# The recurrence's loop on TensorE takes tiles 0 to 13, with an idle turn for the output of a tile that does not exist

## The chip, the cores and the metric

One program runs on one core of one Trainium2 chip. The metric is the device time of the program in microseconds, from start to end, as the median of several runs. TensorE does the matrix products, VectorE, ScalarE and GpSimd the element work, and SyncE (beside GpSimd and ScalarE) issues the transfers. The engines run programs of their own and meet at semaphores.

## The reference

A block of a metaformer: a normalisation over channels, chunked DeltaNet attention, a second normalisation, and a mixture of experts (8 experts, 2 for each token). The change touches the attention's recurrence alone. For each batch and head it is, over chunks of 16 tokens:

```python
def step(S, inp):
    qi, ki, vi, bi = inp
    kk = jnp.einsum('bhid,bhjd->bhij', ki, ki)
    T = eye + jnp.where(strict, bi[..., :, None] * kk, 0.0)
    rhs = bi[..., None] * (vi - jnp.einsum('bhcd,bhde->bhce', ki, S))
    U = jax.scipy.linalg.solve_triangular(T, rhs, lower=True)
    qk = jnp.einsum('bhid,bhjd->bhij', qi, ki)
    O = jnp.einsum('bhcd,bhde->bhce', qi, S) + jnp.einsum('bhij,bhje->bhie', jnp.where(incl, qk, 0.0), U)
    S_new = S + jnp.einsum('bhcd,bhce->bhde', ki, U)
    return (S_new, O)
```

followed by `y = o @ Wo`, and `t + y`. There are 8 batches, 12 heads of 16 channels, and 256 tokens, so 16 chunks.

## The kernel before, in words

The program has three stages. The first normalises, makes keys, values, queries and the triangular matrices, and inverts these. The second is the recurrence, from about 112 to 235 us in the profile below. The third routes the tokens and runs the experts, in 39 units of work of 128 rows.

The recurrence goes over NC = 16 tiles. A tile is one chunk of 16 tokens of all 8 batches, so 128 partitions, and the tiles depend on each other through the state. Each engine has its own loop over the tiles. All but TensorE's are written out by the program that builds the kernel, tile by tile; TensorE's is partly a loop on the engine.

One step of TensorE, `step(c, u, n)` (c the tile, u = c mod 2 the buffer, n = c div 2), does this in order:

- `w_state(c)` (line L1161) takes the state, turned by the triangular inverse, to PSUM bank 5. VectorE subtracts it and writes `uo` (L955).
- `w_and_u(c+1)` (L1131) is the next tile's product with the inverse.
- `turn_o(c-1)` (L1202), two transposes of the former tile's output `ow` into bank 7. ScalarE takes the high part of it as `oTh` (`o_high`, L1049), VectorE the rest as `oTl` (`o_low`, L935).
- `k_u(c)` (L1171) updates the state in banks 0 to 3, which VectorE masks into `s_sb` (L965).
- `output(c)` (L1179, L1185, L1192) makes the tile's output, which ScalarE takes out as `ow` (`o_in`, L1056).
- `turn_w(c+1)` (L1138, from `wx`), then `project(c-1)` (L1215), six products with the output weights `woh` and `wol`, added to the residual by VectorE (`y_in`, L941, and the statistics L944), then `turn_q(c+1)` (L1138, from `qx`).

Most of a step is small fp32 products: 12 in `w_state`, 48 in `w_and_u`, 12 in `k_u`, 12 and 48 in `output`. Each is two weight loads and two matmul instructions in the trace, so a step has 132 x 4 = 528 instructions for these, 30 for the turns, the zeroing product and the projection, and some waits.

Tiles 0 and 1 are written out ahead of the loop, since tile 0 has no former tile: `first(c)` leaves out its `turn_o` and `project`. The loop on the engine takes tiles 2 to 13, two a turn; tiles 14 and 15 are written out behind it. A wait in the loop compares a semaphore with a register that is worked out from the loop's counter.

Beside this, ScalarE and VectorE split the experts' weights into fp16 halves inside the tiles (`expert_high`, `expert_low`; two pieces of VectorE in tile 3, one in the later ones), and GpSimd inverts the second half of the triangular matrices. `wol` is made by GpSimd ahead of that (L861).

Of the kernel before, what the change touches and what calls it, by code (L numbers as in the profile page):

```python
# [22 lines left out]
NC = L // CH  # L23
# [27 lines left out]
WSCALE = 64.0  # L51
# [4 lines left out]
def program(nc, x, consts, wqkvb, wo, gate, wfc, bias, wproj, out):  # L56
# [4 lines left out]
    with ctx:  # L61
# [686 lines left out]
        with ExitStack() as scan:  # L748
# [38 lines left out]
            def o_bank(c):  # L787

                return 6 if isinstance(c, int) and c == NC - 1 else 7

            def rows_of(e):
# [12 lines left out]
            with nc.Block() as block:  # L804
# [88 lines left out]
                def _(dve):  # L893
# [37 lines left out]
                    def o_low(c):  # L931
                        dve.wait_ge(oh_done, c + 1)
                        if c >= 2:
                            dve.wait_ge(y_done, c - 1)
                        nc.vector.tensor_tensor(oTl[c % 2][:, :, :].rearrange("p a n -> p (a n)"), ps[0:HC, o_bank(c), 0:2 * TP],  # L935
                                                oTh[c % 2][:, :, :].rearrange("p a n -> p (a n)"), ALU.subtract)\
                            .then_inc(ol_done, 1)

                    def y_in(c):
                        dve.wait_ge(y_done, c + 1)  # L940
                        nc.vector.scalar_tensor_tensor(r_sb[:, c, :], ps[:, 7, 2 * TP:2 * TP + C], 1.0 / WSCALE, r_sb[:, c, :],  # L941
                                                       ALU.mult, ALU.add).then_inc(y_out, 1)
                        dve.wait_ge(y_out, c + 1)
                        nc.vector.bn_stats(st_sb[:, c, :], r_sb[:, c, :]).then_inc(bn_done, 1)  # L944

                    spread_m(0)
                    nc.vector.memset(s_sb[0][:, :, :, :], 0.0).then_inc(s_ready, 1)
                    spread_m(1)
                    for c in range(NC):
# [40 lines left out]
                def _(act):  # L990
# [54 lines left out]
                    def o_high(c):  # L1045
                        act.wait_ge(o_t, c + 1)
                        if c >= 2:
                            act.wait_ge(y_done, c - 1)
                        nc.scalar.activation(oTh[c % 2][:, :, :].rearrange("p a n -> p (a n)"), ps[0:HC, o_bank(c), 0:2 * TP],  # L1049
                                             ACT.Copy).then_inc(oh_done, 1)  # L1050

                    def o_in(c):
                        act.wait_ge(o_done, c + 1)
                        if c >= 2:
                            act.wait_ge(o_t, c - 1)
                        nc.scalar.activation(ow[c % 2][:, :], ps[:, 5, C:2 * C], ACT.Copy).then_inc(ow_done, 1)  # L1056
# [23 lines left out]

                    nc.scalar.activation(woh[:, :, :], wo_sb[:, :, :], ACT.Copy, scale=WSCALE)
                    nc.scalar.activation(wo_sb[:, :, :], wo_sb[:, :, :], ACT.Copy, scale=WSCALE).then_inc(wo_h, 1)
# [25 lines left out]
                def _(pe):  # L1108
                    def first(c):

                        return isinstance(c, int) and c == 0
# [41 lines left out]
                    def w_state(c, u, n):  # L1153
                        pe.wait_ge(s_ready, c + 1)
                        pe.wait_ge(w_out, c + 1)
                        if not first(c):
                            pe.wait_ge(ow_done, c)
                        for g in range(HG):
                            for bb in range(4):
                                rows = slice(32 * bb, 32 * bb + 32)  # L1160
                                last = nc.tensor.matmul(ps[rows, 5, g * GW:(g + 1) * GW], wT[u][:, g, rows],  # L1161
                                                        s_sb[u][:, bb, g, :], start=True, stop=True)
                        last.then_inc(ws_done, 1)
# [33 lines left out]
                    def turn_o(c, u, n):  # L1197
                        pe.wait_ge(ow_done, c + 1)
                        if not first(c) and o_bank(c) == 7:
                            pe.wait_ge(y_out, c)  # L1200
                        for hf in range(2):
# [4 lines left out]
                    def project(c, u, n):  # L1206
                        pe.wait_ge(ol_done, c + 1)
                        if first(c):
                            pe.wait_ge(wo_l, 1)
                        if o_bank(c) != 7:  # L1210
                            pe.wait_ge(y_out, c)
                        k = 0
# [11 lines left out]
                    def step(c, u, n, more=True):  # L1224
# [4 lines left out]
                        if more:  # L1229
                            w_and_u(*after)  # L1230
                        if not first(c):
                            turn_o(*former)
                        if more:
                            k_u(c, u, n)
                        output(c, u, n)
                        if more:
                            turn_w(*after)
                        if not first(c):
                            project(*former)
                        if more:  # L1240
# [11 lines left out]
                    turn_q(0, 0, 0)  # L1252
                    step(0, 0, 0)
                    step(1, 1, 0)
                    with pe.Fori(1, NC // 2 - 1) as r:
                        step(2 * r, 0, r)
                        step(2 * r + 1, 1, r)
# [566 lines left out]
```

## Time and profile before

| | us |
|---|---|
| median of 3 runs | 450.08 |
| lowest and highest | 446.82, 450.12 |
| the profiled execution | 451.87 |
| its span, first to last instruction | 450.1 |
| what lies around the span | 1.8 |

The profile is of one execution. Its mean granted TensorE clock is 0.860 of full speed. The engines' busy times in it are 373.6 us (83%) for TensorE, 283.4 us (63%) for VectorE, 190.0 us (42%) for ScalarE and 241.7 us (54%) for GpSimd. Times below are microseconds from the span's start. A row of a timeline gives the start, the length, the engine, the line and the operation with its tiles and count; in brackets stands how long the engine was idle ahead of it, and what ended that. "issue" is a wait for nothing that the profile shows.

### The profile page before, as it was taken

To read this page: it belongs to the slowest core of one execution; us is meant where nothing else is said; L and a number is where in the kernel's file an instruction comes from. 1 tells how busy PE (TensorE), PEld (TensorE's weight loads), DVE (VectorE), ACT (ScalarE), POOL (GpSimd) and SP (SyncE) were. 2 spreads that over 40 slices of the span, in tenths; PEclk is the share of its full clock that TensorE was granted. 3 is DMA by queue.
4 is the path that set the end of the run, shared out by engine and by line. 5 is a ranking of instruction groups with operands and counts; after the bars stand their busy time and mean duration, and the time that the engine had idled before them with its cause. 6 is when DMAs were issued, how large, how long until landed. Compare 5 with 4: busy or idle time off the path is not lost. (4 is left out here: it accounts for less than half of the span.)

```text
span 450.1 us, 20125 instructions
## 1 busy us (share of the span) xinstructions
PE 373.6 (83%) x8144; PEld 293.3 (65%) x8144; DVE 283.4 (63%) x627; ACT 190.0 (42%) x444; POOL 241.7 (54%) x285
## 2 busy tenths in 40 slices
PE   3989898873878999999945827899999999999970
PEld 1556666541756787777724513699899998987750
DVE  5696679874445657788655888265756757555440
ACT  4576777421446678777624510133133131321110
POOL 3432336993499615554505303447878778676221
PEclk9998999855865589999985558699999999999895
DMA  7934236493626327787302401214333343334110
GB/s 234 298 134 147 105 119 160 139 275 116 122 82 183 103 77 221 221 250 243 113 1 72 181 35 26 57 28 54 63 58 52 62 58 60 46 44 53 18 22 9
DMA packets 39313, 48.85 MB, mean 109 GB/s; under 512 B 12790, under 2 KB 34886, under 8 KB 39000
## 3 DMA queue, kind: packets, MB, share of 16 engines
q1 hardware_dynamic: 29370, 30.34, 22.2%
q0 software_dynamic: 9488, 16.52, 18.3%
q10 hardware_dynamic: 400, 1.23, 1.0%
q8 instruction: 38, 0.62, 0.6%
q14 instruction: 17, 0.14, 0.1%
HBM read 30.05 MB, written 16.45 MB: 103 GB/s over the span
## 5 line engine op out<-in xcount | busy, mean ns | idle before, releaser
L1750 POOL DMA_INDIRECT out<-yo,give x39 | 68.6, 1759 | 45.7 <-DVE yo L1722 32.6
L1604 PE MATMUL ps<-xs,w_up 128*128 128x256 f16 (+1 forms) x552 | 77.9, 260 | 3.8 <-ACT xb L1663 2.3
L1663 ACT ACTIVATE xb<-xs 64x256 f16<-64x256 f16 (+1 forms) x23 | 8.8, 384 | 127.4 <-DVE xs L1687 127.4
L1604 PEld LDWEIGHTS ps<-xs,w_up 128*128 x552 | 53.1, 98 | 13.7 <-issue 4.9
L1729 POOL DMA_INDIRECT row<-d_x,take x39 | 39.6, 1015 | 33.8 <-DVE take L1451 22.2
L1722 DVE TENSOR_SCALAR yo<-ps,slot_gate 128x192 f32<-128x192 f32 x39 | 14.8, 414 | 51.8 <-PE ps L1624 51.8
L1714 DVE TENSOR_TENSOR hl<-hw,hh 128x512 f16<-128x512 f32 (+1 forms) x69 | 42.3, 614 | 2.4
L1624 PE MATMUL ps<-pjh,hh 128*128 x234 | 42.7, 249 | 0.4 <-DVE hl L1714 0.4
L1624 PE MATMUL ps<-pjh,hl 128*128 x234 | 42.4, 248 | 0.0
L1624 PE MATMUL ps<-pjl,hh 128*128 x234 | 42.4, 248 | 0.0
L1604 PE MATMUL ps<-xb,w_up 66*128 66x256 f16 (+1 forms) x138 | 36.1, 262 | 0.0
L1674 ACT ACTIVATE hw<-ps 128x512 f32<-128x512 f32 (+1 forms) x69 | 31.3, 514 | 7.0 <-PE ps L1604 7.0
L1712 DVE CAST hh<-hw 128x512 f16<-128x512 f32 (+1 forms) x69 | 28.1, 407 | 2.8 <-ACT hw L1674 2.8
L399 POOL TENSOR_TENSOR sqw<-kvw 128x384 f32<-128x384 f32 x8 | 6.6, 828 | 36.2 <-ACT beta L474 29.7
L705 PE MATMUL ps<-kqT 16*32 16x64 f32 x1536 | 20.5, 237 | 4.4 <-issue 3.2
L705 PEld LDWEIGHTS ps<-kqT 16*32 16x32 f32 x1536 | 16.8, 107 | 11.1 <-issue 10.7
L663 PE MATMUL ps<-wqh,tTh 96*128 96x384 f16 (+1 forms) x64 | 21.0, 328 | 3.4 <-DVE tTl L555 1.9
L1624 PEld LDWEIGHTS ps<-pjh,hh 128*128 128x128 f16 x234 | 20.5, 99 | 4.6 <-issue 3.9
L639 PE MATMUL ps<-wqh 96*128 96x512 f16 x49 | 15.9, 458 | 7.3 <-ACT wqh L447 7.3
L935 DVE TENSOR_TENSOR oTl<-ps,oTh 96x256 f16<-96x256 f32 x16 | 6.7, 421 | 23.9 <-ACT oTh L1049 23.9
L1624 PEld LDWEIGHTS ps<-pjh,hl 128*128 128x128 f16 x234 | 21.7, 99 | 0.0
L1624 PEld LDWEIGHTS ps<-pjl,hh 128*128 128x128 f16 x234 | 21.6, 99 | 0.0
(252 smaller groups left out, 939.6 us busy)
## 6 DMA issues: line engine op xcount, KB each, us to landing
d_kv<-kvw SPq DMA_DIRECT2D x8, 384.0 KB, 2.5
d_pt<-w_up SPq DMA_DIRECT2D x16, 192.0 KB, 2.7
kvt<-d_kv SPq DMA_DIRECT2D x16, 192.0 KB, 4.0
pt<-d_pt SPq DMA_DIRECT2D x16, 192.0 KB, 3.6
pjs<-wproj POOLq DMA_DIRECT2D x5, 576.0 KB, 6.6
fcs<-wfc POOLq DMA_DIRECT2D x6, 384.0 KB, 4.9
w_up<-wfc SPq DMA_DIRECT2D x4, 384.0 KB, 5.4
d_q<-qw SPq DMA_DIRECT2D x8, 192.0 KB, 2.7
```

Of the source, the lines that this page charges most:

```text
L639: nc.tensor.matmul(ps[:, bank, :], wqh[:, 0, 0:TP], wqh[:, 0, 0:512], start=True, stop=True)
L663: last = nc.tensor.matmul(ps[:, bank, 0:width], ts[u][:, j, hf, :], ws[:, hf, first:first + width], start=(k == 0), stop=(k == 5))
L705: last = nc.tensor.matmul(ps[cols, 4 + q, 64 * a:64 * a + 64], kqT[j][rows, a, 0, cols], kqT[j][rows, a, :, cols], start=True, stop=True)
L1604: last = nc.tensor.matmul(ps[:, NP * u + m // 2, (m % 2) * n:(m % 2 + 1) * n], w[k][:, m * 128:(m + 1) * 128], x, start=(k == 0), stop=(k ...
L1624: last = nc.tensor.matmul(y[half], hs[u][:, m // 2, at:at + TP], ws[:, m * C:(m + 1) * C], start=False, stop=(m == HB - 1 and k == 2), ski ...
L1663: nc.scalar.activation(xb[s % 2][0:64, 0:width(s)], xs[s % 2][0:64, width(s):2 * width(s)], ACT.Copy).then_inc(xb_in, 1)
L1674: nc.scalar.activation(hw[u][:, i, 0:2 * width(s)], ps[:, NP * u + i, 0:2 * width(s)], ACT.Gelu_apprx_tanh, scale=1.0 / WSCALE).then_inc(h ...
L1712: nc.vector.tensor_copy(hh[u][:, i, 0:n], hw[u][:, i, 0:n]).then_inc(hh_done, 1)
L1714: nc.vector.tensor_tensor(hl[u][:, i, 0:n], hw[u][:, i, 0:n], hh[u][:, i, 0:n], ALU.subtract)\
L1722: nc.vector.tensor_scalar(yo[s % YB][:, half, :], ps[:, 6, half * C:(half + 1) * C], slot_gate[:, at:at + 1], None, ALU.mult).then_inc(yo_ ...
L1729: nc.gpsimd.indirect_dma_start(row[s % RB][:, half, :], None, d_x.rearrange("p t c -> (p t) c"), bass.IndirectOffsetOnAxis(ap=take[:, at:a ...
L1750: nc.gpsimd.indirect_dma_start(out, bass.IndirectOffsetOnAxis(ap=give[:, at:at + 1], axis=0), yo[s % YB][:, half, :], None, compute_op=ALU ...
```

## The change

TensorE's loop takes tiles 0 to 13 in seven turns in place of tiles 2 to 13 in six; nothing of the recurrence is written out ahead of it. So that tile 0 can run the same instructions as the others, it does `turn_o` and `project` for a tile "-1": two transposes of zeros and six products of zeros, whose result nobody reads. VectorE clears `ow[1]`, `oTl[1]` and `oTh[1]` for it ahead of tile 0. Four semaphores start two higher (TURN = 2), and the counts that others wait for on `o_t` and `y_done` are one higher. TensorE waits for the clearing and for `wol` once, ahead of the loop. The order of the work in a step, and all other engines' loops, stay.

```diff
+            oh_clear = of("oh_clear")
+            TURN = 2
...
                     def o_low(c):
                         dve.wait_ge(oh_done, c + 1)
-                        if c >= 2:
-                            dve.wait_ge(y_done, c - 1)
+                        if c >= 1:
+                            dve.wait_ge(y_done, c)
...
                     def y_in(c):
-                        dve.wait_ge(y_done, c + 1)
+                        dve.wait_ge(y_done, c + 2)
...
-                        dve.wait_ge(y_out, c + 1)
+                        dve.wait_ge(y_out, TURN + c + 1)
...
                     nc.vector.memset(s_sb[0][:, :, :, :], 0.0).then_inc(s_ready, 1)
+                    nc.vector.memset(ow[1][:, :], 0.0).then_inc(y_out, TURN)
+                    nc.vector.memset(oTl[1][:, :, :], 0.0).then_inc(ol_done, TURN)
+                    nc.vector.memset(oTh[1][:, :, :], 0.0).then_inc(oh_clear, 1)
                     spread_m(1)
...
                     def o_high(c):
-                        act.wait_ge(o_t, c + 1)
-                        if c >= 2:
-                            act.wait_ge(y_done, c - 1)
+                        act.wait_ge(o_t, c + 2)
+                        if c >= 1:
+                            act.wait_ge(y_done, c)
...
-                        if c >= 2:
-                            act.wait_ge(o_t, c - 1)
+                        if c >= 1:
+                            act.wait_ge(o_t, c)
...
-                    nc.scalar.activation(woh[:, :, :], wo_sb[:, :, :], ACT.Copy, scale=WSCALE)
+                    nc.scalar.activation(woh[:, :, :], wo_sb[:, :, :], ACT.Copy, scale=WSCALE).then_inc(ow_done, TURN)
...
                         pe.wait_ge(w_out, c + 1)
-                        if not first(c):
-                            pe.wait_ge(ow_done, c)
+                        pe.wait_ge(ow_done, TURN + c)
...
                     def turn_o(c, u, n):
-                        pe.wait_ge(ow_done, c + 1)
-                        if not first(c) and o_bank(c) == 7:
-                            pe.wait_ge(y_out, c)
+                        pe.wait_ge(ow_done, TURN + c + 1)
+                        if o_bank(c) == 7:
+                            pe.wait_ge(y_out, TURN + c)
...
                     def project(c, u, n):
-                        pe.wait_ge(ol_done, c + 1)
-                        if first(c):
-                            pe.wait_ge(wo_l, 1)
+                        pe.wait_ge(ol_done, TURN + c + 1)
...
-                        if not first(c):
-                            turn_o(*former)
+                        turn_o(*former)
...
-                        if not first(c):
-                            project(*former)
+                        project(*former)
...
-                    step(0, 0, 0)
-                    step(1, 1, 0)
-                    with pe.Fori(1, NC // 2 - 1) as r:
+                    pe.wait_ge(oh_clear, 1)
+                    pe.wait_ge(wo_l, 1)
+                    with pe.Fori(0, NC // 2 - 1) as r:
                         step(2 * r, 0, r)
                         step(2 * r + 1, 1, r)
```

## Rows read from the trace of the kernel before

**Rows 1.** The page's 40 slices: granted TensorE clock in tenths of full speed.
```profile
PEclk9998999855865589999985558699999999999895
```

**Rows 2.** Stretches cut at clock changes: us, busy (instructions) by engine, PEclk, DMA.
```profile
116.00:122.70 6.70, 5.30 (x221) 4.26 (x224) 2.42 (x4) 4.03 (x12) 2.98 (x5) 1.00 0.64 116
...
129.50:133.00 3.50, 2.65 (x128) 2.00 (x127) 2.26 (x3) 2.55 (x8) 3.34 (x3) 0.99 0.02 5
133.00:160.20 27.20, 24.75 (x715) 20.19 (x715) 16.44 (x25) 15.51 (x35) 20.36 (x22) 0.50 0.45 133
160.30:218.40 58.10, 54.84 (x2672) 44.99 (x2674) 43.53 (x81) 44.16 (x109) 30.12 (x48) 1.00 0.72 215
```

**Rows 3.** Timeline of TensorE in tiles 0 and 1; idle before, and its releaser, in brackets.
```profile
121.49 0.33 PE L1171 MATMUL ps<-uo,kx 32*128 32x64 f32 x3 [0.62 <-issue]
...
124.93 0.69 PE L1138 MATMUL ps<-cst,wx 128*128 128x128 f32 x2 [0.88 <-issue]
126.29 0.88 PE L1138 MATMUL ps<-cst,qx 128*128 128x128 f32 x3 [0.67 <-ACT wT L1035]
...
133.21 0.50 PE L1192 MATMUL ps<-uo,pt 32*32 32x16 f32 x19 [0.94 <-issue]
```

**Rows 4.** Timeline of TensorE in tiles 2 to 5: tile starts and idle places.
```profile
136.07 0.87 PE L1161 MATMUL ps<-s_sb,wT 128*32 128x64 f32 x24
...
139.10 0.64 PE L1131 MATMUL ps<-kvt,mb 32*32 32x32 f32 x28 [1.05 <-issue]
...
144.21 0.84 PE L1192 MATMUL ps<-uo,pt 32*32 32x16 f32 x48 [0.69 <-issue]
...
147.41 0.87 PE L1161 MATMUL ps<-s_sb,wT 128*32 128x64 f32 x24
...
149.49 0.97 PE L1131 MATMUL ps<-kvt,mb 32*32 32x32 f32 x55 [0.49 <-issue]
...
157.25 0.87 PE L1161 MATMUL ps<-s_sb,wT 128*32 128x64 f32 x24
...
164.10 0.54 PE L1161 MATMUL ps<-s_sb,wT 128*32 128x64 f32 x24
```

**Rows 5.** DMA queues carrying instructions: all of them in 136.1:157.25, then in 157.25:218.3.
```profile
q8 instruction: 5, 0.08, 1.6%
...
q14 instruction: 5, 0.04, 0.2%
```

**Rows 6.** Timeline of TensorE in tiles 5 to 7: tile ends and starts at full clock.
```profile
169.59 0.52 PE L1138 MATMUL ps<-cst,qx 128*128 128x128 f32 x3 [0.17 <-ACT wT L1035]
170.20 0.54 PE L1161 MATMUL ps<-s_sb,wT 128*32 128x64 f32 x24
...
175.85 0.52 PE L1138 MATMUL ps<-cst,qx 128*128 128x128 f32 x3 [0.17 <-ACT wT L1035]
176.30 0.54 PE L1161 MATMUL ps<-s_sb,wT 128*32 128x64 f32 x24
```

**Rows 7.** Timeline of TensorE in tile 1: turn and projection of tile 0, at half clock.
```profile
129.33 0.83 PE L1202 MATMUL ps<-cst,ow 128*96 128x128 f32 x2
...
134.34 0.37 PE L1215 MATMUL ps<-woh,oTh 96*128 96x192 f16 x1
...
135.30 0.85 PE L1138 MATMUL ps<-cst,qx 128*128 128x128 f32 x3
```

**Rows 8.** Timeline of VectorE and GpSimd ahead of tile 0.
```profile
112.41 0.70 DVE L947 MEMSET s_sb<- 128x768 f32 x1
...
113.36 1.15 DVE L904 TENSOR_TENSOR mb<-mtc,cst 128x384 f32<-128x384 f32 x1
...
112.35 1.74 POOL L861 TENSOR_TENSOR wol<-wo_sb,woh 96x384 f16<-96x384 f32 x1 [0.52 <-ACT wo_sb L1082]
```

**Rows 9.** Timeline of VectorE in tile 3: the piece that other odd tiles lack.
```profile
154.57 0.94 DVE L918 SCALAR_TENSOR_TENSOR w_up<-w_up 128x768 f16<-128x768 f32 x1
```

**Rows 10.** Timeline of TensorE in the last tile.
```profile
229.66 0.26 PE L1192 MATMUL ps<-uo,pt 32*32 32x16 f32 x9 [1.15 <-issue]
```

More of the change, by code:

```diff
@@ L1206, in project @@
                     def project(c, u, n):
-                        pe.wait_ge(ol_done, c + 1)
-                        if first(c):
-                            pe.wait_ge(wo_l, 1)
+                        pe.wait_ge(ol_done, TURN + c + 1)
                         if o_bank(c) != 7:
-                            pe.wait_ge(y_out, c)
+                            pe.wait_ge(y_out, TURN + c)
                         k = 0
```

## The prediction

> **What bounds the kernel now.** I read the page's clock line first, then stretches of the recurrence cut where the clock changes, then TensorE's timeline tile by tile, then the queues that carry instructions. In the 40 slices the clock shows fives inside the recurrence, in the slices from about 124 to 158 us [rows 1]. The cut stretches give it sharply: full speed from 116.0 to 122.7, full again from 129.5 to 133.0 (half between the two), then half for 27.2 us to 160.2, and full for the remaining 58 us [rows 2]. These are the two levels, 1.2 and 2.4 GHz. TensorE is busy 24.75 of the 27.2 us at half clock and 54.84 of the 58.1 at full, so it is the bound of the recurrence in both, and a tile costs what its instructions cost: 6.10 us at full clock (164.10 to 170.20 to 176.30) [rows 4, 6], but 11.34 for tile 2 and 9.84 for tile 3 [rows 4].
>
> Tiles 2 and 3 hold another thing: three places where TensorE stands still for 1.05, 0.69 and 0.49 us with "issue" as the reason, in the middle of a run of equal products [rows 4]. Tiles 0 and 1 have three such, of 0.62, 0.88 and 0.94 [rows 3]. From tile 4 to tile 13, in the same instructions, I find none. What changes at tile 4 is that the loop on the engine takes its second turn. And the queue named q8, which carries instructions, moves 5 packets during tiles 2 and 3 and none at all during tiles 4 to 13; the 5 packets of that later stretch are q14's, of another size [rows 5]. 0.08 MB in 5 packets is 16 KB each; and between two idle places, 139.10 and 144.21 [rows 4], the timeline has 28 + 2 + 24 + 1 + 24 + 48 = 127 matmuls with as many weight loads, 254 instructions and a few waits. So my reading: the first time TensorE runs through code, it must be brought in block by block, and it waits at the ends of blocks; in later turns the code is there. The change runs tiles 2 and 3 from code that tiles 0 and 1 brought in.
>
> **The change part by part.** I sum against the profiled execution (span 450.1, time 451.87) and carry the difference to the median, 1.79 lower.
>
> *The three waits of tiles 2 and 3 go:* 1.05 + 0.69 + 0.49 = 2.23 us [rows 4]. All of it is on the path, since TensorE runs back to back around them. The waits of tiles 0 and 1 stay, as the first turn now goes through the same number of instructions for the first time; their places move by a few instructions, and I take them at the same 2.44 us in all [rows 3].
>
> *The clock.* Without the waits tile 2 at half clock is 11.34 - 1.74 = 9.60 us, and tile 3 is 9.84 - 0.49 = 9.35; at full it is 6.10, so each tile is about 3.3 us dearer at half. In this trace the clock rose at 160.3, 10.8 us after the last of the idle places ended at 149.49, with TensorE busy without a break in between [rows 2, 4]. That is the one row that tells how soon it rises in this sort of work, and I take it: the last idle place of the first turn ends near 133.9 (133.21 and 0.7 for the idle turn below), so the clock rises near 144.7. Tile 2 starts at 136.07 + 0.7 = 136.8 and does 7.9 of its 9.60 us at half, the rest (18%) at full in 1.1, and ends at 145.8. Tile 3 runs at full: 6.1, and 0.9 because there VectorE becomes late: it has one more piece of expert weights (0.94 us) than in the other odd tiles, where it has no slack left [rows 9]. That ends at 152.8, and tile 4 at 158.9. Before, tile 5 began at 164.10 [rows 4]. That is 5.2 us earlier, with the 2.23 and the 0.7 in it. Bounds: clock at full from the start of tile 2 gives 136.8 + 6.1 + 7.0 + 6.1 = 156.0, so 8.1 earlier; clock rising at 160.3 as before gives 136.8 + 9.60 + 9.35 = 155.75, then 4.55 us at half (48% of a tile) and 3.15 at full, so 163.45 and 0.65 earlier.
>
> *The idle turn in tile 0.* Two transposes: 0.83 us at half clock in tile 1 [rows 7], and as they stand in tile 0 behind `w_and_u`, near 120 and thus at full clock [rows 2], half of it, 0.4. They delay `k_u` and all behind it. The six products take 135.30 - 134.34 = 0.96 us at half clock [rows 7]; in tile 0 they fall into the 0.67 us in which TensorE waits for ScalarE's `wT` [rows 3], so 0.3 is left. Together 0.7, between 0.4 (products hidden) and 1.8 (nothing hidden, all at half).
>
> *Three clearings on VectorE.* The one of `s_sb`, four times the size of `ow`, takes 0.70 us [rows 8]; so three at less than 0.25 each, 0.7 at most. They push `spread_m(1)`, which ends at 114.51 [rows 8] and is wanted by `w_and_u(1)` behind the 0.54 us of `w_state(0)` at about 118.7. Four us of slack hide them. If that cover were gone they would cost their 0.7. Nobody else is queued behind them before tile 0; SyncE's loads of the inverse for tile 3 wait for `mb_done` and are wanted two tiles later.
>
> *Waits ahead of the loop.* TensorE now waits for `wol` before tile 0, and all of the recurrence is queued behind that. `wol` is done at 112.35 + 1.74 = 114.09 [rows 8] and TensorE gets there at 118.2, so it costs nothing; it would from 4.1 us of lateness on. `ow_done`'s first count comes from ScalarE's very first operation. The waits of ScalarE and VectorE name one count more and start from one more: the same moments.
>
> *One more jump back.* From tile 5 to 6, with a jump between, 0.61 us pass between the start of the last turn and the next tile; from 6 to 7, without, 0.45 [rows 6]. So +0.16 for the seventh turn's jump; the set-up of the counter moves from ahead of tile 2 to ahead of tile 0 at no price.
>
> *Behind the recurrence.* TensorE's program is two tiles shorter, so all later block ends fall elsewhere. One wait of this kind, 1.15 us, lies in the last tile, where nothing covers it [rows 10]: it may vanish, or another come. I count 0, and 1.2 either way for the range. What follows (statistics, routing) waits for the last tile's residual, so the gain goes through to the end.
>
> The Trainium skill, Runtime: NRT & Kernel Launch, section Instruction fetch mechanics, gives TensorE 2048 instructions in blocks of 256, which agrees with the 16 KB packets and idle places here, but calls the crossing of a block "mostly hidden". By that rule the 2.23 us would be no waits for code and would not go, and the sum would be a small loss; the rows differ, with up to 1.05 us at a crossing. The same section warns that a taken branch whose target is outside a window of two blocks forces a new fetch. The trace disagrees: the loop spans more than four blocks, and its jumps bring no packet.
>
> Sum: -5.2 + 0.16 = -5.0 on the span. 451.87 - 5.0 - 1.79 = **445.1 us**.
>
> **The rivals.**
> *The clock rises early, or never falls.* For it: at 129.5 it rose while idle places of 0.88 and 0.67 lay only 3 to 5 us back [rows 2, 3]. Against: 27 us at half with small waits only. -8.1 + 0.16 = -7.9: 442.2.
> *The clock rises when it did before.* For it: tiles 3 and 4 kept TensorE busy for 10 us and it stayed at half. Only 0.65 - 0.16 = 0.5 is left: 449.6.
> *The waits are not of the code's first pass,* or come again in tiles 2 and 3. Then nothing goes and the idle turn and the jump stay: +0.9, 451.0. Against: the packets of q8 [rows 5].
> *The clock is lost in tiles 0 and 1 too.* This is the one on the slower side. Before, 4.5 us of tile 0 (118.2 to 122.7) and 3.5 of tile 1 ran at full [rows 2]; at half they cost 8.0 x 9.5 / 6.1 = 12.4, so 4.4 more. With a rise as late as after tile 4, tile 5 begins at 136.8 + 4.4 + 9.60 + 9.35 + 9.35 = 169.5, or 5.4 later: with the jump +5.6, 455.6. It decides once the half clock holds from tile 0 beyond the middle of tile 4; up to there the gain covers it. For it: the idle turn leaves the waits of the first tiles as they are. Against: it adds work where TensorE stood idle.
> *Every turn fetches its code again.* This is the skill's branch rule as a mechanism of this kernel: the loop's first block has been overwritten at the jump. Each of the six later turns would have the 2.23 us: 13.4 - 2.2 + 0.9 = +12, 462. Against: the five jumps of before, over the same body, moved nothing on q8 [rows 5]. Only the place of the block ends in the body differs.
>
> **How the numbers follow.** Forecast 0.45; early clock 0.20; clock as before 0.20; waits stay 0.05; clock lost 0.07; fetched again 0.03. The range of 441.5 to 450.8 takes in the first four with the tail's 1.2 at most of them, and leaves out the last two and some ends. A difference under 1%, 4.5 us, can hardly be told from none. The forecast itself is on the faster side of that in 0.6 of its cases: faster 0.27 + 0.20 = 0.47; slower 0.10; the rest, 0.43, within 1%.
>
> **What would show it.** Right: no "issue" over 0.2 us in tiles 2 to 13, q8 silent from the first jump on, the same two or three idle places in tiles 0 and 1, the clock at full some 11 us after the last of them, tile 5 near 159. In tile 0 two transposes and six products that cost under 1 us together. Wrong: idle places in tile 2, packets on q8 in later turns, or a clock that stays at half past 150. Then the sign may still be right but the size not. A clock that differs from run to run would make the one profile a poor guide to the median.

## The result, and the profile after

The changed kernel took 448.14 us in the median of 20 runs (445.03 to 451.34), the one before 450.33 in 20 runs of its own (446.82 to 453.75). The ratio is 0.9954, with an interval of 0.9932 to 0.9976: faster, by 1.9 us in the profiled executions (450.01 against 451.87) and by 2.2 in the medians. Forecast were 5.0. The sign was right, and the time lies inside the range; the size was not. At half a per cent the difference is also below the 1% that the prediction called hardly to be told from none; that it is real rests on the same sign in four pairs of kernels (below).

The timeline of TensorE in the changed kernel, tile starts (`w_state` is now at L1165) and idle places, answers to [rows 3, 4]:

```profile
117.66 0.87 PE L1165 MATMUL ps<-s_sb,wT 128*32 128x64 f32 x24
...
124.69 0.29 PE L1196 MATMUL ps<-uo,pt 32*32 32x16 f32 x4 [1.53 <-issue]
...
130.88 0.42 PE L1136 MATMUL ps<-kvt,mb 32*32 32x32 f32 x11 [1.35 <-issue]
...
138.08 0.87 PE L1165 MATMUL ps<-s_sb,wT 128*32 128x64 f32 x24
...
145.92 0.54 PE L1165 MATMUL ps<-s_sb,wT 128*32 128x64 f32 x24 [0.76 <-DVE s_sb L970]
...
148.35 0.63 PE L1206 MATMUL ps<-cst,ow 128*96 128x128 f32 x2 [0.92 <-DVE r_sb L943]
...
155.18 0.87 PE L1165 MATMUL ps<-s_sb,wT 128*32 128x64 f32 x24
...
162.16 0.54 PE L1165 MATMUL ps<-s_sb,wT 128*32 128x64 f32 x24
...
216.41 0.54 PE L1165 MATMUL ps<-s_sb,wT 128*32 128x64 f32 x24
```

And in the kernel before, the starts of tile 0 and tile 14:

```profile
118.23 0.54 PE L1161 MATMUL ps<-s_sb,wT 128*32 128x64 f32 x24
...
218.37 0.54 PE L1161 MATMUL ps<-s_sb,wT 128*32 128x64 f32 x24
```

From tile 2 to tile 13 no idle place with the reason "issue" is longer than 0.22 us: the 2.23 us are gone. In tile 3 TensorE now waits for VectorE instead, 0.76 us at its start for the masked state and 0.92 for the residual. The tile lengths are what is new: tiles 0 and 1 took 138.08 - 117.66 = 20.42 us, and before 136.07 - 118.23 = 17.84. Tiles 2 and 3 took 17.10 against 21.18 [rows 4]. From the start of tile 0 to that of tile 5 it is 44.50 us against 45.87, so 1.4 us of gain, where the forecast has 5.2.

The queues that carry instructions, in tiles 2 to 13 (answers to [rows 5]), have nothing of q8 left:

```profile
q14 instruction: 5, 0.04, 0.2%
```

The stretches of the changed kernel, cut at tile 2 and where the clock changes (stretch, its us, busy and count for TensorE, its loads, VectorE, ScalarE, GpSimd, then granted clock, DMA share and GB/s), answer to [rows 2]:

```profile
117.70:138.10 20.40, 17.51 (x562) 14.47 (x561) 7.56 (x12) 9.47 (x25) 18.08 (x19) 0.58 0.26 66
138.10:148.20 10.10, 8.39 (x400) 6.91 (x399) 6.66 (x9) 8.89 (x20) 9.78 (x10) 0.84 0.80 241
148.20:158.40 10.20, 10.05 (x289) 8.19 (x292) 7.86 (x13) 5.40 (x16) 7.85 (x8) 0.50 0.21 59
158.50:216.40 57.90, 54.84 (x2664) 45.05 (x2663) 43.37 (x81) 43.87 (x108) 30.57 (x48) 1.00 0.74 216
```

The granted clock was at 0.58 of full over tiles 0 and 1 (0.72 before), at full from 141.4 to 148.2 (0.84 over that row), at half again for ten us in which TensorE was busy 10.05 of 10.20 us, and then full to the end of tile 13. Before, the 27.2 us at half were one piece. So the clock did come up earlier, 10.5 us after the last idle place ended at 130.88, much as forecast. What the forecast did not have is that it fell again, beside the waits for VectorE. That these brought it down is argued from their place, not shown.

VectorE in tiles 2 to 4 of the changed kernel:

```profile
142.06 0.42 DVE L937 TENSOR_TENSOR oTl<-ps,oTh 96x256 f16<-96x256 f32 x1 [2.63 <-ACT oTh L1054]
142.40 1.27 DVE L900 TENSOR_TENSOR mtc<-mtc,beta 128x192 f32<-128x192 f32 x1
143.70 1.22 DVE L906 TENSOR_TENSOR mb<-mtc,cst 128x384 f32<-128x384 f32 x1
144.84 0.94 DVE L970 TENSOR_TENSOR s_sb<-ps,cst 128x768 f32<-128x768 f32 x1
145.71 0.96 DVE L924 SCALAR_TENSOR_TENSOR w_up<-w_up 64x768 f16<-64x768 f32 x1
146.59 1.34 DVE L926 SCALAR_TENSOR_TENSOR pjl<-pjl,pjh 128x1152 f16<-128x1152 f32 x1
147.86 0.34 DVE L943 SCALAR_TENSOR_TENSOR r_sb<-ps,r_sb 128x192 f32<-128x192 f32 x1
...
148.52 0.34 DVE L960 TENSOR_TENSOR uo<-ub,ps 128x192 f32<-128x192 f32 x1
...
151.91 1.34 DVE L920 SCALAR_TENSOR_TENSOR w_up<-w_up 128x768 f16<-128x768 f32 x1
...
156.41 0.34 DVE L960 TENSOR_TENSOR uo<-ub,ps 128x192 f32<-128x192 f32 x1
```

In tile 2 it stands idle for 2.63 us until `oTh` is there. Then it spreads the triangular matrices (`mtc` and `mb`, 1.27 and 1.22 us) before it comes to the state, which TensorE waits 0.76 us for. Behind that stands one expert piece of two parts (0.96 and 1.34 us), and only then the residual, which TensorE waits 0.92 us for. So `uo` of tile 3 comes at 148.5, 2.6 us after the tile's start; in the later tiles the same takes 0.7 to 1.7 (from 162.16 to 162.83 in tile 5). Both waits in tile 3 thus stand behind VectorE's work of tile 2, which itself began late because of `oTh`. The extra piece in tile 3 (1.34 us at 151.91), which the prediction had priced, held TensorE up by nothing that shows.

The last two tiles are the other place of the difference. From the start of tile 14 to the reciprocal behind the statistics pass 232.05 - 216.41 = 15.64 us, before 235.21 - 218.37 = 16.84. First the reciprocal of the changed kernel, then that of the kernel before:

```profile
232.05 0.25 DVE L991 RECIPROCAL rstd<-rstd 128x16 f32<-128x16 f32 x1 [0.37 <-ACT rstd L1110]
```

```profile
235.21 0.25 DVE L986 RECIPROCAL rstd<-rstd 128x16 f32<-128x16 f32 x1 [0.37 <-ACT rstd L1105]
```

The 1.15 us of [rows 10] are gone, and tile 14 is as long as it was (6.77 and 6.82). By the reciprocal the changed kernel is 3.16 us ahead, 0.57 of it from ahead of tile 0 and 2.6 from the recurrence; 1.26 us of it are lost again in the routing stage, ahead of the gate's scores, where the one long piece is a transfer: the chain that ended last holds it at `d_x`, 3.69 us in the changed kernel and 1.61 before, at the same spot. First the chain of the changed kernel (start, us, what):

```profile
246.28 3.69 DMA d_x<-x
```

The same chain of the kernel before:

```profile
250.53 1.61 DMA d_x<-x
```

I take that for chance of the one execution: from the reciprocal to the end of the span it is 215.9 us in this profile, 214.2 in the second profile of the same kernel, and 214.9 and 215.3 in the two of the kernel before. What is said below of sizes goes by medians.

### The profile page after: what moved, and what is told of

Same layout as the page of the kernel before. It is cut to its first block and busy times, and to the rows that moved or that the text cites. A ratio compares the mean times of both kernels' runs of the same rounds, so it can differ in the third digit from the quotient of the medians.

```text
span 448.0 us, 20168 instructions
## 1 busy us (share of the span) xinstructions
PE 372.3 (83%) x8152; PEld 292.9 (65%) x8152; DVE 285.3 (64%) x630; ACT 189.9 (42%) x444; POOL 244.0 (54%) x285
## 3 DMA queue, kind: packets, MB, share of 16 engines
q0 software_dynamic: 9488, 16.52, 18.6%
## 5 line engine op out<-in xcount | busy, mean ns | idle before, releaser
L639 PE MATMUL ps<-wqh 96*128 96x512 f16 x49 | 16.9, 481 | 7.2 <-ACT wqh L447 7.2
```

The lines of the kernel that those rows point to most:

```text
L639: nc.tensor.matmul(ps[:, bank, :], wqh[:, 0, 0:TP], wqh[:, 0, 0:512], start=True, stop=True)
```

## The experiments

All ratios are to the kernel before on the same chip. The table has the medians; the columns of tiles are us in the one profiled execution of each, from tile start to tile start, "tail" is from the start of tile 14 to the reciprocal behind the statistics, and "all" is from the start of tile 0 to that reciprocal (tiles 6 to 13, not shown, take 48.0 to 48.5 us in every kernel). In names, +64, +128 and +192 are instructions of padding, explained below. The profiled execution need not be a typical one: it was the fastest of its runs, 2 to 5 us under the median, in the second profile of before, "four tiles written out", +192, "+128, piece later" and "piece earlier".

| kernel | median | ratio (95%) | tiles 0, 1 | 2, 3 | 4, 5 | tail | all |
|---|---|---|---|---|---|---|---|
| before | 450.33 | | 17.84 | 21.18 | 12.95 | 16.84 | 116.98 |
| before, second profile | 451.07 | 1.0041 (1.0011 to 1.0071) | 18.90 | 18.98 | 12.25 | 17.37 | 115.65 |
| after | 448.14 | 0.9954 (0.9932 to 0.9976) | 20.42 | 17.10 | 13.16 | 15.64 | 114.39 |
| after, again | 446.89 | 0.9925 (0.9895 to 0.9955) | 20.28 | 17.09 | 12.49 | 16.25 | 114.18 |
| idle turn alone | 451.50 | 1.0036 (1.0007 to 1.0064) | 20.05 | 18.95 | 12.74 | 17.92 | 117.75 |
| four tiles written out | 456.87 | 1.0149 (1.0096 to 1.0202) | 18.68 | 19.04 | 19.51 | 16.52 | 122.22 |
| after, piece later | 446.26 | 0.9926 (0.9890 to 0.9961) | 20.70 | 15.21 | 12.39 | 16.13 | 112.50 |
| after, 12 products | 447.16 | 0.9957 (0.9923 to 0.9990) | 20.67 | 16.78 | 12.42 | 16.02 | 113.95 |
| before, 12 products | 450.03 | 1.0013 (0.9984 to 1.0042) | 20.49 | 18.78 | 12.88 | 17.38 | 117.68 |
| after, +64 instructions | 447.23 | 0.9934 (0.9905 to 0.9964) | 18.43 | 15.82 | 13.16 | 17.84 | 113.33 |
| after, +128 | 445.63 | 0.9915 (0.9888 to 0.9942) | 15.29 | 13.41 | 15.31 | 19.22 | 111.28 |
| after, +192 | 448.29 | 0.9974 (0.9940 to 1.0007) | 17.81 | 15.17 | 13.15 | 15.34 | 109.53 |
| before, +128 | 450.39 | 1.0025 (0.9989 to 1.0062) | 16.11 | 22.68 | 12.95 | 15.69 | 115.60 |
| after, +128, piece later | 444.21 | 0.9873 (0.9830 to 0.9917) | 14.75 | 15.51 | 12.75 | 17.06 | 108.16 |
| after, piece earlier | 445.22 | 0.9924 (0.9892 to 0.9955) | 20.38 | 14.91 | 12.58 | 15.31 | 111.36 |
| after, piece earlier, +128 | 444.29 | 0.9903 (0.9869 to 0.9937) | 14.73 | 14.52 | 12.57 | 18.66 | 108.64 |

The second profile of before is the very same program, and came out 0.4% off itself with an interval that leaves out 1. So I take differences of under about half a per cent between two of these kernels for undecided, whatever their intervals. The sign of the change does not hang on one such difference: after against before is worth 0.46%, 0.75%, 0.56% (both with 12 products) and 1.1% (both with +128), and "all" is 114.39 and 114.18 us against 116.98 and 115.65.

### The changed kernel again

> The changed kernel itself once more, beside the kernel before. Theory (waits for code removed, part of the gain spent again): ratio 0.995, between 0.992 and 0.998, no idle place with reason issue above 0.3 us in tiles 2 to 13. Rival (the difference of the two profiles is where the clock happened to change, nothing of the program): ratio 1.000.

0.9925. With the first measurement the change is worth 0.5 to 0.75%, 2 to 3.4 us. In tiles 2 to 13 no idle place with the reason "issue" is over 0.2 us, and TensorE waits 1.49 us for VectorE's state at the start of tile 3. The rival (ratio 1.000) is out.

### The idle turn alone

```diff
-                    with pe.Fori(0, NC // 2 - 1) as r:
+                    step(0, 0, 0)
+                    step(1, 1, 0)
+                    with pe.Fori(1, NC // 2 - 1) as r:
```

> The changed kernel with tiles 0 and 1 written out again ahead of the loop, so that only the idle turn and the shifted counts are left of the change. Theory: the waits of tiles 2 and 3 are back (3 places, 2 to 2.5 us in all, 5 packets on q8 in tiles 2 and 3), and the idle turn costs 0.4 to 1 us: ratio 1.001 to 1.003. Rival (the idle turn itself costs the 2.6 us that tiles 0 and 1 grew by in the one profile): ratio 1.006. Rival (the gain came from the counts or the idle turn, not the loop): ratio 0.995.

1.0036. By this ratio the idle turn costs about 1.6 us (0.3 to 2.9). That is under the half per cent that I call undecided, and the interval also takes in the rival's 1.006, so the size of this cost is not settled. Tiles 0 and 1 took 20.05 us, about as long as in the changed kernel. The waits of tiles 2 and 3 are back, one of them much longer than in the profile of before.

TensorE's timeline of this kernel in tile 2:

```profile
140.50 0.52 PE L1136 MATMUL ps<-kvt,mb 32*32 32x32 f32 x37 [1.06 <-issue]
...
146.01 0.98 PE L1196 MATMUL ps<-uo,pt 32*32 32x16 f32 x58 [2.56 <-issue]
```

Taken at its face, the rest of the change, the loop from tile 0, is worth 1.0036 - 0.9954 to 1.0036 - 0.9925, 0.8 to 1.1% or 3.7 to 5.0 us, and a good third of it is given back by the idle turn. The last tiles are in that sum too: this kernel has their idle places (1.38 us at 228.8), the changed one doesn't.

### Four tiles written out

```diff
                     step(0, 0, 0)
                     step(1, 1, 0)
-                    with pe.Fori(1, NC // 2 - 1) as r:
+                    step(2, 0, 1)
+                    step(3, 1, 1)
+                    with pe.Fori(2, NC // 2 - 1) as r:
```

> The kernel before with tiles 0 to 3 written out and the loop on tiles 4 to 13: the suspected cost once more. Theory: tiles 4 and 5 now hold idle places of about 2.2 us in all, 4 or 5 more packets on q8, and the clock stays at half longer: tiles 4 and 5 take 16 to 21 us in place of 12.95, so 3 to 8 us more, ratio 1.007 to 1.018. Rival (waits come from the first tiles' data, not from code run for the first time): tiles 4 and 5 stay near 13 us, ratio 1.000.

1.0149, 6.7 us more, and tiles 4 and 5 at 19.51 in place of 12.95 and 12.25. Here is the suspected cost in a place where there was none before. TensorE's timeline of this kernel in tiles 4 and 5, the idle places:

```profile
155.31 0.89 PE L1131 MATMUL ps<-kvt,mb 32*32 32x32 f32 x82 [1.03 <-issue]
...
159.22 0.31 PE L1185 MATMUL ps<-s_sb,qT 128*32 128x64 f32 x6 [1.32 <-issue]
...
166.86 0.45 PE L1171 MATMUL ps<-uo,kx 32*128 32x64 f32 x8 [0.83 <-issue]
...
170.41 0.23 PE L1192 MATMUL ps<-uo,pt 32*32 32x16 f32 x2 [1.30 <-issue]
```

Its queue q8 in tiles 4 and 5:

```profile
q8 instruction: 4, 0.07, 1.4%
```

And in tiles 6 to 13:

```profile
q8 instruction: 1, 0.02, 0.1%
```

Four idle places with 4.48 us in all, 4 packets, then a single packet over eight tiles (at 185.8, with no wait at it over 0.24 us). That the waits belong to the first pass through code, and not to the first tiles' data, is shown. Their price in this profile is 4.5 us of idle time and some 2 us that go with the clock, which fell at 161.2 and 168.0.

### A piece of VectorE's work in another tile

```diff
-                        return {0: (), 1: (0,), 2: (1,), 3: (2, 3)}.get(c, (c,))
+                        return {0: (), 1: (0,), 2: (1,), 3: (3,), 12: (2, 12)}.get(c, (c,))
```

The count that piece 2 gave is given by piece 3.

> The changed kernel with one of VectorE's two pieces of expert weights in tile 3 done in tile 12, where VectorE waits 1.9 us (it then splits weights that are no longer there, so one part of expert 1's weights is not the reference's). Theory (VectorE late in tiles 3 and 4 gives back part of the gain, 0.94 us directly, and its waits on TensorE let the clock fall again): 1 to 3 us less than the changed kernel, ratio to before 0.988 to 0.993. Rival (VectorE's lateness is a one-off of the profiled execution, since TensorE at half clock covers it): same as the changed kernel, 0.995.

0.9926: against the changed kernel's 0.9925 on the same chip that is nothing. Tiles 2 and 3 took 1.9 us less in the profile, but the medians (446.26 and 446.89) differ by 0.6 only. Undecided by itself. The edit also misses the waits it was meant for: those stand in tile 3 and come from VectorE's work of tile 2, and they are still there, 0.83 and 0.70 us. What is shorter in this profile went with the clock, 0.84 over tiles 2 and 3 against 0.70.

### Twelve products that keep TensorE warm

```diff
                     batch_steps(pe, step)
+                    keep_busy(2, 12)
```

> The changed kernel with 12 products of 512 columns on TensorE behind its last work of the first stage, where it stood idle for 6 us, so that it comes warm into tile 0. If the clock in tiles 0 and 1 holds much of the time: tiles 0 and 1 take 17.5 to 18.5 us in place of 20.3, and the ratio to before is 0.985 to 0.990. Rival (the waits for code set the pace of tiles 0 and 1 whatever the clock): 19.5 to 20.5 us, ratio 0.992 to 0.995.

> The kernel before with the same 12 products. If the clock in tiles 0 to 3 is what such work buys: ratio 0.990 to 0.995, and tiles 0 and 1 at 16 to 17 us. Rival (as the waits for code pull the clock down again within a tile): ratio 1.000. The difference of this run and the changed kernel with the same products is what the change is worth from a warm start: theory 0.005 to 0.010 of the ratio.

0.9957 and 1.0013: the products buy nothing in either kernel, against what I expected. Tiles 0 and 1 took 20.67 and 20.49 us. The clock was up at 113.0 and fell at 119.8 in the one, up at 114.2 and down at 121.0 in the other, just behind idle places of 1.19 and 1.33 us in tile 0.

TensorE's timeline of the changed kernel with them, in tiles 0 and 1:

```profile
119.27 0.89 PE L1176 MATMUL ps<-uo,kx 32*128 32x64 f32 x19 [1.19 <-issue]
...
123.09 0.41 PE L1197 MATMUL ps<-uo,pt 32*32 32x16 f32 x16 [0.72 <-issue]
...
129.34 0.39 PE L1137 MATMUL ps<-kvt,mb 32*32 32x32 f32 x23 [1.86 <-issue]
```

It is not shown by this that the clock follows the waits for code. With +128 and the later piece (below) tiles 0 and 1 had four idle places, of 0.23, 0.79, 0.43 and 0.93 us, and the clock stayed at full throughout. A stretch of it, from where the clock rose to where it fell:

```profile
115.30:142.40 27.10, 21.38 (x990) 17.07 (x991) 14.23 (x23) 19.99 (x50) 23.48 (x25) 1.00 0.43 103
```

Nor was a warm start really tried. The kernel before came into tile 0 at full clock without the products too: the clock rose 2.3 us ahead of it in the first profile (115.9 for 118.23) and 2.4 in the second, and 2.5 with the products. In the changed kernel it rose 2.6 us ahead with them; without them 2.5 ahead in the second profile, and 3.2 us late in the first (120.9 for 117.66). With the products added to both, the change is worth 0.6%.

### Where the block ends fall

```diff
                     batch_steps(pe, step)
+                    for _ in range(64):
+                        nc.tensor.matmul(ps[:, 2, 0:8], wqh[:, 0, 0:TP], wqh[:, 0, 0:8], start=True, stop=True)
```

Each such product is a weight load and a matmul. 32, 64 and 96 of them move the block ends by a quarter, a half and three quarters of 256 instructions; they run where TensorE stood idle for 6 us.

> The changed kernel with 64 small products (128 instructions, half a block of 256) in the same idle stretch, so that all later block ends fall half a block earlier in the work. Theory: the idle places of the first turn move by half a block and keep their sum of 2.5 to 3.5 us, the time moves by less than 1 us: ratio 0.991 to 0.996. Rival (where the block ends fall decides the cost of tiles 0 and 1, and the change had bad luck with it): tiles 0 and 1 move by 1.5 us or more either way. If the places don't move, blocks of 256 instructions are not what they are.

0.9915, and tiles 0 and 1 in 15.29 us, the rival's case, not mine. The timeline of their idle places:

```profile
118.97 0.61 PE L1138 MATMUL ps<-kvt,mb 32*32 32x32 f32 x47 [0.22 <-issue]
...
122.71 0.75 PE L1198 MATMUL ps<-uo,pt 32*32 32x16 f32 x68 [1.06 <-issue]
...
132.92 0.54 PE L1167 MATMUL ps<-s_sb,wT 128*32 128x64 f32 x24 [0.41 <-DVE s_sb L972]
```

Two idle places of 1.28 us in all are left of four block ends, and the clock was at 0.89 of full over both tiles. Of the 5.1 us against 20.42, 1.6 are idle time (2.88 to 1.28); the rest went with the clock (0.58 to 0.89). But tiles 4 and 5 took 15.31 us, with TensorE waiting 1.94 us for VectorE, and the last two 19.22 in place of 15.6, with the clock at half from 213.9.

Its timeline of TensorE in tiles 3 and 4:

```profile
141.58 0.40 PE L1208 MATMUL ps<-cst,ow 128*96 128x128 f32 x2 [0.96 <-DVE r_sb L945]
...
149.76 0.40 PE L1208 MATMUL ps<-cst,ow 128*96 128x128 f32 x2 [1.94 <-DVE r_sb L945]
```

> The changed kernel with 32 small products (64 instructions, a quarter of a block) in TensorE's idle stretch between the stages. Theory (where the block ends fall sets the cost of tiles 0 and 1 and of the last two tiles): tiles 0 and 1 between 15.3 us (half a block) and 20.4 us (none), ratio 0.988 to 0.996. Rival (the small products help by keeping the clock up, not by moving the ends): as with 64 products, 15 to 16 us.

0.9934, tiles 0 and 1 at 18.43, the tail at 17.84: between the two, as the theory has it. The idle time in tiles 0 and 1 isn't between the two, though: 0.60, 2.42 and 0.90 us, 3.92 in all, with the clock at 0.78.

> The changed kernel with 96 small products (192 instructions, three quarters of a block) at the same place. Theory: tiles 0 and 1 again at 16 to 20 us, since the ends are a quarter of a block from the unpadded places. Rival (small products keep the clock up): 15 us or less, ratio below 0.990.

0.9974, tiles 0 and 1 at 17.81 although this one has the most products. That speaks for the place of the ends and against the products' warmth, with one profile at each padding. This one was of a lucky execution (443.27 us, with the median at 448.29) and says little more.

> The kernel before with 64 small products (128 instructions). If the ends of blocks are what counts, the kernel before gains in tiles 0 and 1 as the changed one did, 3 to 5 us, or loses it again in tiles 2 and 3, which have their own four ends: ratio 0.990 to 1.003. Then the change itself, both with 64 products, is worth 0.3 to 1%. Rival (the gain with the padding belongs to the changed kernel alone): ratio 1.000 and tiles 0 and 1 at 18.5 us.

1.0025. The kernel before gained 1.7 and 2.8 us in tiles 0 and 1 (16.11 us against 17.84 and 18.90), less than the 3 to 5 that I expected and than the changed kernel's 5, and lost 1.5 and 3.7 in tiles 2 and 3 (22.68 against 21.18 and 18.98), which in it are first passes too.

TensorE's timeline of it in tiles 2 and 3, the waits for code:

```profile
138.06 0.43 PE L1187 MATMUL ps<-s_sb,qT 128*32 128x64 f32 x16 [1.44 <-issue]
...
149.64 1.33 PE L1173 MATMUL ps<-uo,kx 32*128 32x64 f32 x17 [3.71 <-issue]
...
153.46 0.40 PE L1194 MATMUL ps<-uo,pt 32*32 32x16 f32 x12 [0.20 <-issue]
```

One wait for code here is 3.71 us. In the changed kernel tiles 2 and 3 hold no such wait at any of the paddings. From the two with +128 the change is worth 1.1%.

### The padding and the later piece together

> The changed kernel with 64 small products and with VectorE's second piece of tile 3 done in tile 12 (one part of expert 1's weights is not the reference's). With 64 products alone TensorE waited 3.3 us for VectorE in tiles 3 and 4. Theory (once TensorE is quick there, VectorE is the bound): tiles 2 to 5 take 1.5 to 3.5 us less than the 28.7 with the products alone, ratio 0.984 to 0.989. Rival (VectorE has no slack later either and the piece only moves): same as with 64 products, 0.9915.

0.9873, the lowest ratio of all. Against +128 alone (0.9915) that is 0.4%, and the intervals overlap; it has 6 runs, and its profile is of the fastest of them. In the profile the wait for VectorE in tile 4 is gone (12.75 us for tiles 4 and 5), but tiles 2 and 3 took 15.51 with the clock at half from 142.5 to 149.3, so that tiles 2 to 5 are only 0.5 us shorter than with +128 alone, where I expected 1.5 to 3.5. That VectorE limits tiles 3 and 4 is seen in the timelines; what it costs is not settled by this.

### The kernel before, once more

> The kernel before as it is, for a second profile of it. If the one profile on which the forecast rested was an unlucky one for the clock: tiles 2 and 3 take 18 to 20 us and not 21.2, with the clock up for some stretch between 133 and 160 us. Otherwise: 21 us and half clock throughout. Ratio 1.000 either way.

Tiles 2 and 3 took 18.98 us, not 21.2. The clock in them, cut at the tile starts:

```profile
135.00:143.20 8.20, 7.59 (x284) 6.27 (x287) 4.77 (x9) 6.86 (x16) 8.04 (x9) 0.71 0.66 189
143.20:154.00 10.80, 8.78 (x282) 7.23 (x282) 6.42 (x11) 5.42 (x14) 10.02 (x11) 0.66 0.42 136
154.00:160.00 6.00, 5.83 (x281) 4.86 (x280) 4.63 (x10) 4.72 (x13) 2.52 (x3) 0.95 0.13 32
```

0.71, 0.66 and then 0.95, where the first profile has 0.50 for 27.2 us [rows 2]. The same two tiles took 19.04, 18.95 and 18.78 us in the three other kernels without padding that run them for the first time (four tiles written out, idle turn alone, before with 12 products). The profile on which the forecast rested was the worst of five for the clock. The executions without a trace kept say the same: over the 114 of the kernel before that were measured beside the experiments, the mean granted clock of the program had a median of 0.871, and only 8 were as low as the 0.860 of that profile.

### The complete kernel with the piece moved

```diff
-                        return {0: (), 1: (0,), 2: (1,), 3: (2, 3)}.get(c, (c,))
+                        return {0: (), 1: (0,), 2: (), 3: (3,)}.get(c, (c,))
...
                                                 ALU.subtract).then_inc(u_done, 1)
+                        if c in (2, 3):
+                            expert_low(c - 1)
                         if c:
                             o_low(c - 1)
```

> The changed kernel, complete, with VectorE's pieces of expert weights of tiles 2 and 3 moved ahead of o_low, where VectorE waited 2.6 us for oTh (piece 1 in tile 2, piece 2 in tile 3). Theory (VectorE's lateness in tiles 3 and 4 holds TensorE up by 1.7 us and lets the clock fall): tiles 2 to 5 at 28 to 29 us in place of 29.6 to 30.3, ratio 0.990 to 0.993. Rival (the pieces ahead of o_low only make oTl late instead): ratio 0.994 to 0.996.

0.9924. Tiles 2 to 5 took 27.5 us against 30.25 and 29.58 in the two profiles of the changed kernel, and the clock fell just for 3.5 us (143.7 to 147.2). The wait for the residual in tile 3 is gone (0.58 us of it stand in tile 4), the one for the state is 1.19 us. But this is the profile of its fastest execution, 3.0 us under its median, and in the time the ratio is 0.3% under the first measurement of the changed kernel and equal to the second: a gain is not shown.

> The same with 64 small products that move the block ends by half a block. Theory: both gains add up, as with the piece moved to tile 12: tiles 2 to 5 at 26 to 28 us in place of 28.7, ratio 0.986 to 0.990, faster than both kernels. Rival (with TensorE quick, the piece ahead of o_low delays oTl and so the projection): 0.991 or above.

0.9903 (444.29 us): of the kernels that compute everything this is the fastest measured, and its interval ends at 0.9937, clear of the kernel before. From the changed kernel (0.9954, with an interval down to 0.9932, and 0.9925) and from +128 alone (0.9915) it isn't told apart. Tiles 2 to 5 took 27.1 us; the last two tiles lose 2.4 to 3 us again, with an idle place of 1.00 us between the first two products of the projection (up to 214.2) and the clock at half from 214.3.

## Why the prediction was right or wrong

*The three waits go, 2.23 us, with no packet of q8 in the later turns:* right. Four tiles written out brought them to tiles 4 and 5, and the changed kernel has none over 0.22 us in tiles 2 to 13, with the ends in four different places. Not every block end makes TensorE wait: 5 packets of q8 go with the three waits of tiles 2 and 3 [rows 4, 5]. The rule of the Trainium skill (Runtime: NRT & Kernel Launch, Instruction fetch mechanics) is that the crossing of a block is mostly hidden. In first passes here it often is not: idle places there were 0.2 to 3.7 us. The Trainium skill's rule in the same section, that a taken branch out of the current window forces a fetch, did not show either: in both profiles of the changed kernel six jumps went back over a body of more than four blocks, and q8 moved no packet. Three of the other kernels had one packet of q8 in a later turn (+192 at 150.9, before with +128 at 168.3, four tiles written out at 185.8), each within 1 us of a jump, and none with a wait over 0.24 us.

*The clock:* this term is the one that failed most. I had 5.2 us for tiles 2 to 4 with the waits and the idle turn in it, of which some 3.7 were the clock. It was taken from a profile in which the clock was at half for 27.2 us, and I treated that as the kernel's state. Four other profiles of the same two tiles had 18.8 to 19.0 us for them and not 21.2, so most of the gain that I counted was never there to be had. From those 19.0 to 17.1 are 1.9 us, just about the waits: the clock over these tiles was 0.68 and 0.70. In the changed kernel's own profile the step "tile 3 runs at full", and tile 4 after it, is what failed: the clock rose at 141.4, even before the 144.7 of the forecast, and fell back to half at 148.2 for ten us. Tiles 2 to 4 took 24.1 us (7.84, 9.26 and 6.98) where I had 22.1. The second part of the error is that VectorE took the place of the removed waits. I had put it at 0.9 us in tile 3, from the extra piece of that tile; it was 1.7 at the start of tile 3 and 1.5 in the second profile, from VectorE's work of tile 2 (the matrices ahead of the state, an expert piece ahead of the residual), which I hadn't looked at. How much of the clock's fall is due to these waits stays open.

*The idle turn, 0.7 us:* this term failed too, by less. It is 1.6 by the kernel with it alone (0.3 to 2.9), near the upper bound of 1.8, and in the profiles tiles 0 and 1 grew by more, from 17.8 and 18.9 to 20.1 to 20.7 in all kernels with it and no padding. I priced its instructions, not what becomes of a stretch that waits for code: in the profile of before the two tiles had 2.44 us of waits and the clock at 0.72, in the changed kernel 2.88 and 3.54 us, at 0.58 and 0.69. The growth need not be the idle turn as such. The kernel before with 12 products has no idle turn, and took 20.49 us for the same tiles, and with +128 the kernels with the idle turn took less (14.7 to 15.3) than before without it (16.11). How the cost divides between instructions, places of the ends and the clock stays open.

*Block ends behind the loop, counted at 0 with 1.2 either way:* a gain of 1.2 in the first profile, 0.6 to 1.1 in the second against either of before; and up to 3.6 us of loss with other ends (19.22 against 15.64). The bound was too tight, and the larger part of this risk lay in tiles 0 and 1, where I wrote that the places "move by a few instructions" and took the cost as fixed: it went from 20.4 to 15.3 us with half a block, two thirds of that with the clock.

*Covered things* (clearings of 0.22, 0.17 and 0.17 us, the wait for `wol`) cost nothing that shows. Three semaphores start two higher (`y_out`, `ol_done`, `ow_done`), not four, which changes nothing of this. The jump's 0.16 us: in the changed kernel 0.69 us pass there (167.65 to 168.34) in place of 0.61, which is made up elsewhere in the turn: tiles 6 to 13 took 48.07 us, and 48.17 before.

The sum of the parts: loop 3.7 to 5.0 us gained, the last two tiles' ends among them, idle turn 1.6 lost, which gives 2.1 to 3.4. That the sum comes out is no check, since both parts were taken from the same ratios. Of what was gained, 0.6 to 1.2 us came from the last two tiles, which the forecast counted at 0: that much of it is luck. And the range of 441.5 to 450.8 takes in 450.08, no change at all, so that the time lies inside it says little.

## What to carry to other kernels

One profile shows one history of the clock: before a gain is priced from a stretch at half clock, look at a second profile, or price it at both levels and let the forecast sit at the near end. Look at the time of the profiled execution beside the median, and at its mean granted clock beside those of the other runs. Where code is run for the first time on TensorE, count instructions to the next block end and see what stands there: work added in such a stretch, or ends moved by half a block, changed tiles 0 and 1 by up to 5 us here. What one stretch gains by it another can lose (3.6 us in the last two tiles, and in the kernel before all of it), so judge it by the whole time. When a wait is taken out, walk the engine that comes next through the same tiles, one by one, from the tile ahead of them on, since the first of them may have other work than the later ones.

## What the runs showed of the hardware

The price of one block end in a first pass varied from nothing to 3.71 us between these kernels. Of the four waits over 2 us three (2.39, 2.56, 3.71) fell in tiles 2 and 3, where the DMA engines carry more: their mean busy share during these waits was 0.94, 0.98 and 0.72. But during the fourth (2.42, in tile 1 with +64) it was 0.09, and a wait of 0.69 us in tile 2 of before had 0.93. Over all 66 idle places of 0.2 us and more with the reason "issue" in tiles 0 to 5 of the sixteen profiles, length and DMA share hardly go together (a correlation of 0.22). So that the fetch of code queues behind data is possible for the longest; it was not tried by itself, and does not explain the others.

Code once run stayed: in both profiles of the changed kernel q8 moved no packet while the loop ran six more times over some 1120 matmuls and weight loads. The single packets of three other kernels are told above.

The clock fell from full to half within 1 us behind an idle place of 1.2 to 1.3 us in tile 0 of both kernels with 12 products added. It did not fall at four idle places of 0.23 to 0.93 us in tiles 0 and 1 with +128 and the later piece. The 12 products were worth nothing measurable (0.9957 and 1.0013), and the clock was at full at the start of tile 0 in both profiles of before without them.
